# A graph layer and an eight-expert feed-forward layer on one core: 128-row blocks in pairs, five groups of tiles, biases inside the weights

## The reference, cut to what matters

```python
def _layernorm(x, axis=-1, eps=1e-05):
    m = jnp.mean(x, axis=axis, keepdims=True)
    v = jnp.var(x, axis=axis, keepdims=True)
    return (x - m) / jnp.sqrt(v + eps)
...
        h = layer_norm(x, ln_gamma, ln_beta)
        agg = jnp.einsum('bij,bjh->bih', adj, h)
        conv = jnp.einsum('bkh,ho->bko', agg, W_rel) + b_rel + jnp.einsum('bkh,ho->bko', h, W_root)
        return x + jax.nn.relu(conv)
...
        gate_scores = jnp.einsum('bsd,ed->bse', x, Wg) + bg
        topk_scores, topk_idx = jax.lax.top_k(gate_scores, K)
        topk_probs = jax.nn.softmax(topk_scores, axis=-1)
        combine = jnp.sum(topk_probs[..., None] * jax.nn.one_hot(topk_idx, E, dtype=x.dtype), axis=-2)
        out = jnp.zeros_like(x)
        for e in range(E):
            h = jax.nn.relu(jnp.einsum('bsd,hd->bsh', x, W1[e]) + b1[e])
            y = jnp.einsum('bsh,dh->bsd', h, W2[e]) + b2[e]
            out = out + combine[..., e:e + 1] * y
        return out
    x = x + _L0_gnn_ref(_layernorm(x, axis=-1), adj, L0_gnn_W_rel, L0_gnn_b_rel, L0_gnn_W_root, L0_gnn_ln_gamma, L0_gnn_ln_beta)
    x = x + _L0_ffn_ref(_layernorm(x, axis=-1), L0_ffn_Wg, L0_ffn_bg, L0_ffn_W1, L0_ffn_b1, L0_ffn_W2, L0_ffn_b2)
```

## Time and profile before

| | us |
|---|---|
| median of 3 runs | 629.91 |
| lowest and highest run | 625.02, 630.95 |
| span of the profiled execution | 878.1 |
| busy in it: PE, DVE, POOL, ACT | 471.1, 385.6, 272.6, 237.7 |

### The profile page before, as it was taken

The page is one execution under the profiler, slowest core; times in us unless marked ns, Lnnn a source line. Parts: engine busy times, 40 slices in busy tenths (PEclk is TensorE's granted clock), DMA queues, the critical chain, the costliest instruction groups (busy, mean ns, idle before and its releaser), DMA issues.

```text
span 878.1 us, 14976 instructions
## 1 busy us (share of the span) xinstructions
PE 471.1 (54%) x4776; PEld 395.1 (45%) x4777; DVE 385.6 (44%) x1146; ACT 237.7 (27%) x467; POOL 272.6 (31%) x268
## 2 busy tenths in 40 slices
PE   0613243441799997401099997201299951899500
PEld 0613233330688886201088886100188840688400
DVE  2979933830454667200044668000055620456622
ACT  0413100210356554000056553000044410344200
POOL 3053373067000000777400001777300067000274
PEclk9955575565799999655589999655599975899955
DMA  9980012011112112211112112111122222221341
GB/s 346 416 287 1 19 51 64 6 58 51 43 44 78 56 57 67 68 54 51 33 44 78 57 57 82 52 54 51 27 73 72 72 78 53 74 73 54 135 132 57
DMA packets 32173, 70.78 MB, mean 81 GB/s; under 512 B 14458, under 2 KB 14714, under 8 KB 31364
## 3 DMA queue, kind: packets, MB, share of 16 engines
q1 hardware_dynamic: 21520, 37.66, 13.0%
q0 software_dynamic: 8192, 16.79, 6.6%
q10 hardware_dynamic: 2420, 15.77, 4.4%
HBM read 32.45 MB, written 37.75 MB: 80 GB/s over the span
## 4 chain that ended last, share of the span: by engine, by line
PE 42%; issue 20%; another core or an unknown queue 13%; DVE 13%; DMA 4%; ACT 3%; POOL 3%; SPq 2%; ACTq 0%; DVEq 0%; POOLq 0%
PE PH L876 14%; PE PY L893 13%; PE PH L872 5%; POOL YG L311 3%; DMA ADJ<-in_adj 3%; PE PX L859 2%; ACT N L695 1%; PE PY L886 1%; SPq L223 1%; ACT N L677 1%; PE PA L824 1%; DVE VARN L377 1%; DVE MDIF L376 1%; DVE N L442 1%
## 5 line engine op out<-in xcount | busy, mean ns | idle before, releaser
L298 POOL DMA_INDIRECT rows<-XHL,IDX x128 | 123.2, 962 | 347.1 <-DVE IDX L515 309.3
L540 DVE SCALAR_TENSOR_TENSOR HL<-PH,HH 128x512 f16<-128x512 f32 x192 | 129.8, 689 | 207.0 <-ACT HH L726 114.1
L726 ACT ACTIVATE HH<-PH 128x512 f16<-128x512 f32 x192 | 113.6, 596 | 263.1 <-PE PH L876 107.9
L311 POOL DMA_INDIRECT YG<-yrows,IDX x128 | 121.3, 948 | 202.7 <-DMA yrows<-YB 164.3
L876 PE MATMUL PH<-XT,W1H 128*128 128x256 f16 x768 | 144.3, 281 | 22.8 <-issue 22.6
L893 PE MATMUL PY<-W2H,HL 128*128 x768 | 131.0, 223 | 31.8 <-issue 31.8
L893 PE MATMUL PY<-W2H,HH 128*128 x768 | 131.1, 223 | 25.3 <-issue 25.3
L893 PE MATMUL PY<-W2L,HH 128*128 x768 | 109.3, 223 | 42.1 <-issue 42.1
L535 DVE COPY XT<-PX 128x512 f16<-128x512 f16 x96 | 40.5, 422 | 168.6 <-issue 63.1
L876 PE MATMUL PH<-XT,W1L 128*128 128x256 f16 x384 | 107.8, 281 | 12.3 <-issue 12.3
L876 PEld LDWEIGHTS PH<-XT,W1H 128*128 x768 | 76.3, 100 | 55.8 <-issue 32.9
(11 more groups left out here) (154 smaller groups left out, 559.8 us busy)
## 6 DMA issues: line engine op xcount, KB each, us to landing
rows<-XB ACTq DMA_DIRECT2D x4, 3072.0 KB, 29.8
XB<-rows SPq DMA_DIRECT2D x32, 384.0 KB
yrows<-YB SPq DMA_DIRECT2D x32, 384.0 KB, 2.3
out<-X SPq DMA_DIRECT2D x16, 256.0 KB
X<-in_x SPq DMA_DIRECT2D x3, 1024.0 KB, 28.2
YG<-in_w ACTq DMA_DIRECT2D x1, 2048.0 KB, 9.6
ADJ<-in_adj SPq DMA_DIRECT2D x32, 64.0 KB, 3.8
YG<-in_w SPq DMA_DIRECT2D x1, 2048.0 KB, 29.7
```

What stands on the lines that cost most here:

```text
L298: nc.gpsimd.indirect_dma_start(rows[q], bass.IndirectOffsetOnAxis(ap=IDX[:, col:col + 1], axis=0), XHL[:, src:src + 2 * P].bitcast(F32), N ...
L311: nc.gpsimd.indirect_dma_start(YG[q % 2][:, dst:dst + P], None, yrows[q], bass.IndirectOffsetOnAxis(ap=IDX[:, col:col + 1], axis=0)).then_ ...
L540: nc.vector.scalar_tensor_tensor(HL[:, at:at + 2 * BW], PH[h][:, :], 0.0, HH[:, at:at + 2 * BW], ALU.max, ALU.subtract).then_inc((loa_made ...
L726: nc.scalar.activation(HH[:, at:at + 2 * BW], PH[h][:, :], ACT.Relu).then_inc((hia_made, hib_made)[h][j], 1)
```

## The change: what it does, and its diff

The whole kernel is written anew around the same arithmetic.

- Blocks have 128 rows. An expert's slots are padded to whole blocks of 128. Two blocks form a pair, and each block of a pair has its own expert number (two value_loads for each pair). A group of m tiles has 2m + 8 blocks.
- The tiles form five groups of 8, 16, 16, 16 and 8 tiles, with 24, 40, 40, 40 and 24 blocks: 168 blocks, 84 pairs, instead of 96 blocks of 256 rows.
- The hidden layer of a pair has 24 matmuls of 128 columns and no bias matmul; its output has 2 bias matmuls and 24 others, all of 128 columns.
- The bias b1 is folded into the weights: a normalised row sums to zero, so its last feature is replaced by a constant 1, every weight row has the last row subtracted, and the last row becomes the bias. b_rel, bg, gamma and beta are folded in the same way (AF, WF). residual is one DVE instruction instead of two.
- The weights are folded and split by PE and ACT: for each of 16 pieces of 512 columns PE multiplies in float32 (twice for W1, once for W2), ACT writes the high part, PE subtracts it, ACT writes the low part. POOL does no arithmetic any more.
- Graph quads 0 to 5 (groups 0 and 1) run before the first pair, in three lots of two. Quads 6 to 15 run between the pairs, each over six pairs from the one in START. Statistics, routing and combine have their pairs in STATS, ROUTE and COMBINE. Group 1 is routed in pairs 0 to 3.
- The order of POOL is scatter 0, 1, gather 0, scatter 2, 3, gather 1, scatter 4, gather 2, 3, 4, with 16 indirect DMAs for a group of 8 tiles and 32 for one of 16: 128 and 128 in all, as before.
- Nothing is in a loop of the hardware; all 84 pairs are written out on every engine. xT_copy is on ACT. ACT issues the stores of results. SP loads rows in chunks of 4 blocks into a ring of 4, and the adjacency tiles of later quads between these loads.
- Two row buffers are filled with zeros instead of four (2.6 MB each).

In the PE list, pair p is: rows_transpose(p+1), hidden(p), then xn_transpose or relation of a quad, output(p-1), then score, convolve or h0_transpose of a quad.

```diff
+GS = (8, 16, 16, 16, 8)
+G = len(GS)
...
+NS = [2 * s + E for s in GS]
+S0 = [sum(NS[:g]) for g in range(G + 1)]
+P0 = [s // 2 for s in S0]
+NP = P0[G]
...
+XR, YR = 4, 3
...
+START = {6: 2, 7: 5, 8: 8, 9: 11, 10: 15, 11: 19, 12: 23, 13: 27, 14: 32, 15: 37}
+STATS = {2: 0, 3: 9, 4: 27}
+ROUTE = {1: 0, 2: 17, 3: 33, 4: 43}
+COMBINE = {0: 24, 1: 26, 2: 60, 3: 62, 4: 64, 5: 66, 6: 78, 7: 80, 8: 82, 9: 83}
...
+            def load_rows(ch):
+                g, c = chunk_cols(ch)
+                if 2 * ch == P0[g]:
+                    sp.wait_ge(scattered[g], 2 * GS[g] * 16)
+                if ch >= XR:
+                    sp.wait_ge(xT_done, 2 * (ch - XR) + 2)
+                sp.dma_start(XB[:, ch % XR * CW:(ch % XR + 1) * CW], rows_p[g][:, c]).then_inc(xb_in[ch % XR], 16)
...
+            for ch in range(NC):
+                load_rows(ch)
+                for n, at in START.items():
+                    if ch == at // 2 + 2:
+                        sp.wait_ge(conv_done, n - 3)
+                        load_adj(n)
...
             scatter(0)
             scatter(1)
+            gather(0)
             scatter(2)
-            gather(0)
             scatter(3)
             gather(1)
+            scatter(4)
             gather(2)
             gather(3)
...
+            gather(4)
...
+            def residual(n):
+                dve.wait_ge(conv_done, n + 1)
+                dve.wait_ge(sum_made, n + 1)
+                xv = X[:, n * GW:(n + 1) * GW]
+                nc.vector.scalar_tensor_tensor(xv, banks(n)[0][:, :], 0.0, xv, ALU.max, ALU.add).then_inc(conv_read, 1)
+                dve.wait_ge(conv_read, n + 1)
...
+            for p in range(NP):
+                for n, at in START.items():
+                    if p == at + 5:
+                        split_low(n)
+                        scores(n)
+                    if p == at + 2:
+                        residual(n)
+                    if p == at + 3:
+                        scales_out_first(n, 1)
+                    if p == at + 4:
+                        scales_out_last(n, 1)
+                low_half(p, 0)
+                low_half(p, 1)
+                for n, at in START.items():
+                    if p == at + 2:
+                        stats_out(n, 0)
+                for g, at in STATS.items():
+                    for i in range(GS[g] // GT):
+                        if p == at + i // 2:
+                            stats_in(g, i)
+                    if p == at + 2:
+                        scales_in_first(g)
+                        scales_in_last(g)
+                for g, at in ROUTE.items():
+                    if p == at:
+                        route_first(g)
+                    if p == at + 1:
+                        route_second(g)
+                    if p == at + 2:
+                        route_slots(g)
+                        route_rows(g)
+                    if p == at + 3:
+                        route_blocks(g)
+                for n, at in COMBINE.items():
+                    if p == at:
+                        combine(n)
...
+            def weight_whole(c):
+                if c >= 3:
+                    pe.wait_ge(wlo_made, c - 2)
+                w = slice(c % E * HID, (c % E + 1) * HID)
+                if c < E:
+                    nc.tensor.matmul(WB[c % 3][:, :], KF[:, K_M:K_M + P], YG[0][:, w], start=True, stop=False)
+                    nc.tensor.matmul(WB[c % 3][:, :], KF[0:1, K_E:K_E + P], B1R[0:1, w], start=False, stop=True).then_inc(w_done, 1)
...
+                    nc.tensor.matmul(WB[c % 3][:, :], ident, YG[1][:, w], start=True, stop=True).then_inc(w_done, 1)
...
+                nc.tensor.matmul(WB[c % 3][:, :], KH[:, neg:neg + P], hi[:, c % E * HID:(c % E + 1) * HID],
+                                 start=False, stop=True, skip_group_check=True).then_inc(w_rest, 1)
...
+            def hidden(p, es):
+                pe.wait_ge(xT_made, p + 1)
...
+                    if p:
+                        pe.wait_ge((loa_made, lob_made)[h], p)
+                    for t in range(2):
+                        hi, lo = XT[:, at + t * P:at + (t + 1) * P], XT[:, at + BW + t * P:at + BW + (t + 1) * P]
+                        for c in (2 * h, 2 * h + 1):
+                            o = PH[h][:, c % 2 * BW + t * P:c % 2 * BW + (t + 1) * P]
+                            wh = W1H[:, bass.ds(es[t] * C + c * P, P)]
+                            wl = W1L[:, bass.ds(es[t] * C + c * P, P)]
+                            nc.tensor.matmul(o, wh, hi, start=True, stop=False)
+                            nc.tensor.matmul(o, wh, lo, start=False, stop=False)
+                            last = nc.tensor.matmul(o, wl, hi, start=False, stop=True)
+                    last.then_inc((ha_done, hb_done)[h], 1)
...
+            def output(p, es):
+                pe.wait_ge(loa_made, p + 1)
+                pe.wait_ge(lob_made, p + 1)
+                if p >= 2:
+                    pe.wait_ge(y_made, p - 1)
+                for t in range(2):
+                    py = PY[p % 2][:, t * P:(t + 1) * P]
+                    nc.tensor.matmul(py, KH[:, H_B2M:H_B2M + P], B2[:, bass.ds(es[t], P)], start=True, stop=False)
+                    for c in range(C):
+                        at = (p % 2 * C + c) * BW + t * P
+                        wh = W2H[:, bass.ds(es[t] * C + c * P, P)]
+                        wl = W2L[:, bass.ds(es[t] * C + c * P, P)]
+                        nc.tensor.matmul(py, HH[:, at:at + P], wh, start=False, stop=False)
+                        nc.tensor.matmul(py, HL[:, at:at + P], wh, start=False, stop=False)
+                        last = nc.tensor.matmul(py, HH[:, at:at + P], wl, start=False, stop=c == C - 1)
+                last.then_inc(y_done, 1)
```

More of the change, by code:

```diff
@@ L274, in _ @@
+            for n in range(NQ):
+                if n not in COMBINE or COMBINE[n] // 2 + 6 >= NC:
+                    store_out(n)
+            sp.wait_ge(out_done, NQ * 16)
         @block.gpsimd
@@ new lines, in _ @@
+            for n in (0, 1):
+                u_copy(n)
+            for n in (0, 1):
+                plus_norm(n)
+            split_weights(0)
+            for n in (0, 1):
+                split_high(n)
+            for n in (0, 1):
+                xnT_copy(n)
+            act.wait_ge(b2_zero, 1)
+            act.wait_ge(b2_in, 32)
+            nc.scalar.activation(B2[0:1, :], B2F[0:1, :], ACT.Copy, scale=YS / 64.0).then_inc(b2_made, 1)
+            nc.scalar.activation(BT[32:33, :], B2F[32:33, :], ACT.Copy, scale=YS / 64.0).then_inc(bt_made, 1)
@@ L810, in h0_transpose, with relation @@
                 last.then_inc(h0T_done, 1)
-            def relation(k, bank, there):
-                pe.wait_ge(hT_made, there)
-                for t in range(GT):
-                    last = nc.tensor.matmul(tile(bank, t), tile(T4, k * GT + t), WREL[:, :], start=True, stop=True)
+            def relation(n):
+                pe.wait_ge(hT_made, n + 1)
+                for k in range(GT):
+                    last = nc.tensor.matmul(tile(banks(n)[1], k), tile(quad(T4, n), k), WF[:, 0:P], start=True, stop=True)
@@ L817, in relation, with convolve @@
                 last.then_inc(u_done, 1)
-            def convolve(k, bank, there, loaded):
-                pe.wait_ge(u_made, there)
-                pe.wait_ge(adj_in[k], loaded)
-                for t in range(GT):
-                    nc.tensor.matmul(tile(bank, t), tile(T4, k * GT + t), WROOT[:, :], start=True, stop=False)
-                    last = nc.tensor.matmul(tile(bank, t), tile(ADJ, k * GT + t), tile(U4, k * GT + t), start=False, stop=True)
+            def convolve(n):
+                pe.wait_ge(u_made, n + 1)
+                pe.wait_ge(adj_in[n % 4], 32 * (n // 4 + 1))
+                for k in range(GT):
+                    o = tile(banks(n)[0], k)
+                    nc.tensor.matmul(o, tile(quad(T4, n), k), WF[:, P:2 * P], start=True, stop=False)
+                    last = nc.tensor.matmul(o, tile(quad(ADJ, n), k), tile(quad(U4, n), k), start=False, stop=True)
@@ L826, in convolve, with xn_transpose @@
                 last.then_inc(conv_done, 1)
[L828 to L831 removed]
+            def xn_transpose(n):
+                pe.wait_ge(xn_made, n + 1)
+                for k in range(GT):
+                    last = nc.tensor.transpose(tile(banks(n)[2], k), tile(quad(N4, n), k), ident)
                 last.then_inc(xnT_done, 1)
[L834 to L838 removed]
@@ new lines, in _ @@
+            nc.tensor.matmul(PA[:, 2 * P:2 * P + E], KF[0:1, K_E:K_E + P], KF[0:1, K_BG:K_BG + E], start=False, stop=True).then_inc(fold_done, 1)
+            pe.wait_ge(wf_made, 1)
+            for n in (0, 1):
+                h0_transpose(n)
+            for n in (0, 1):
+                relation(n)
+            for n in (0, 1):
+                convolve(n)
+            pe.wait_ge(w1_in, 16)
+            pe.wait_ge(b1_in, 16)
+            pe.wait_ge(kh_in, 16)
+            split_weights(0)
```

(20 more changed lines are left out.)

1286 lines of the change are left out of this document (617 added, 669 removed).

## The result

The changed kernel takes **670.85 us** (median of 5 runs, 664.52 to 675.8) against 629.43 for the kernel before beside it (5 runs): a ratio of **1.062**, with a 95% interval of 1.055 to 1.068. It is slower; 532 us was predicted, and the range ended at 585. A second time, on other runs, it took 665.06, ratio 1.056 (1.052 to 1.061). Some executions of a kernel are slower than its others at a lower granted clock (2 of the first 5 runs here, 1 of the second 5); medians are of all runs, ratios and intervals leave these out.

A forecast was written before the change was run, and what follows sets the result against it. PE's blocks were taken to pace the kernel before, POOL's queue to bound the changed one's end. The sum: 165 to pair 9's wait, plus 142.5 is 307.5, plus 201.6 is 509, end 520, with 12 carried over 532 us; range 492 to 585.

The forecast's parts named there:

- A pair: Each pair's work on PE without a quad: hidden matmuls at 0.056 us, the rest unchanged; 3.01 us, 84 pairs 253.
- Start: Everything before pair 0, with the first graph quads and weight folding: pair 0 at 95 us (bounds 86 and 112).
- pairs 0 to 3: First pairs, where DVE's added work holds PE back: 24.5 us including pipeline filling, slots of group 1 at 119.5.
- the new wait: In pair 9, PE's convolve(8) waits for an adjacency tile queued behind scatter 1's rows: 15 us, until 165.
- Quads between pairs: From pair 9 to group 3's slots in pair 35: 6.4 us a quad, 142.5 in all (bounds 123 and 175).
- POOL from there: From scatter 3 on, POOL issues 160 indirect DMAs and finds each input ready: 201.6 us, to 509; POOL bounds the end.
- The 12 us carried over: Unexplained gap between the kernel before's summed terms, 618, and its timed median, added to the forecast (bounds 0 and 25).
- The standstill: Five stretches in the kernel before's profile, all engines but POOL nearly still, 268.5 us: claimed absent from timed runs.
- Rival (d): Standstills beside POOL's trains of indirect DMAs belong to straight code, not the profiler: 713 us; chance 0.06.
- Rival (c): In the pairs, a 128-column product with weights from a register's address costs above 0.056 us: 565, at the bound 608; chance 0.12.
- (b): Graph and experts mesh better between pairs: DVE's additions hide and pair 0 is at 86; sum 504 us; chance 0.15.
- (e): No gain: DVE and ACT both fall behind in the pairs, 5.9 us for each of 84: 633 us; chance 0.03.

The follow-up runs named there:

- h1: The changed kernel with every slot on expert 0 (no loads, constant addresses), timed where the kernel before took 629.53: 537.16 us, ratio 0.853.
- e1: The changed kernel with every slot on expert 0 (no loads, constant addresses), timed where the kernel before took 880.14: 792.93 us, ratio 0.900.
- e3: The changed kernel with both loads per pair kept but unused and constant matmul addresses, where the kernel before took 880.14: 812.72 us, ratio 0.923.

## Why the prediction was wrong

| Step | predicted | changed kernel | pairs without a choice (h1) |
|---|---|---|---|
| first hidden product | 95 | 101.15 | 92.96 |
| scatter 1 begins | 119.5 | 128.92 | 119.83 |
| wait for the tile in pair 9 ends | 165 | 174.54 | 165.31 |
| scatter 3 begins | 307.5 | 353.62 | 319.85 |
| POOL's last DMA is issued | 509 | 657.8 | 521.7 |
| span | 520 | 669.0 | 533.0 |
| time | 532 | 670.85 | 537.16 |

**The step that failed is "A pair", 3.01 us.** It priced "24 matmuls of 128 columns" by L893's 0.056 and held that "the rest is unchanged". The columns were right to 0.01 us.
The term's size carries the miss. h1 takes it away and comes to 537 against 671, 134 us less. That is fewer than 84 x 2.8 = 235, since in h1 POOL's queue takes over as the bound at 320, as the prediction had it, and, as I read it (no run shows it by itself), since part of a pair's extra time lies beside waits that pairs with quads have anyway.

**Start, pairs 0 to 3, the new wait:** right where the stream isn't the bound (h1 within 2.1 us at each of the three), which is partly luck: e1, the same file, has its first hidden product at 109.03, h1 at 92.96. In the changed kernel they come 6 to 10 us later; what part of that is the stream in pairs 0 to 8 and what the start, which differed by 6 us between two traces of the changed kernel itself (101.15 and 107.53), I can't say. The price of the wait itself was 15; it measured 10.9 in h1 and 3.9 in the changed kernel.

**Quads between pairs:** from the wait to scatter 3, 142.5 predicted, 154.5 in h1 (319.85 - 165.31), inside the bounds of 123 to 175; 12 too few, which is most of what h1's span has over 520.

**POOL from there:** right in h1, wrong in the changed kernel. POOL waits 76.08 us before gather 3 and 22.69 before its last one, for results that PE hasn't made:

```profile
575.36 0.94 POOL L293 DMA_INDIRECT YG<-yrows,IDX  x1 [76.08 <-DMA yrows<-YB]
...
637.93 1.12 POOL L293 DMA_INDIRECT YG<-yrows,IDX  x1 [22.69 <-DMA yrows<-YB]
...
656.84 0.94 POOL L293 DMA_INDIRECT YG<-yrows,IDX  x1 [0.30 <-issue]
```

**The 12 us carried over:** around a span lie 1.9 us, not 12. The 10 too many and the 12 missing at the quads cancel, so that h1 comes as near to 532 as it does is luck in part.

**The standstill** was misread as the profiler's. It made no large error in the sum, since its stretches were taken out, but the expectation that the profile after would show them failed. Rival (d) fails too: they aren't tied to straight code, and none took part in the 671.

**Rival (c)** came closest: a product "whose weights come from a register's address costs more". Its mechanism was put in the product, and its bound, 0.11 us for each of 24, gave 608. The cost lies in the instructions ahead of the products and in the loads, in output as much as in hidden, and it has no bound in the products' own rows. **Rivals (b) and (e)** fall: ACT and DVE don't bound the pair, e1's 3.02 has the same work on them.

## What to carry to other kernels

Before splitting a product's block so that each half has its own run-time address, list what TensorE's stream gets per block: matmuls, register instructions, loads. Here 18 register instructions and one load per 256 rows were free behind 3.4 us of columns, and some twice that cost 2.8 us; the padding saved (84 pairs for 104 blocks) was worth less. When the trace shows an instruction that starts late and names a semaphore of another engine, and the gap is the same at each step, ask what stands ahead of it in its own stream. And before building on a profile, compare its span with the times: here they told of two conditions of the chip, of which one adds 250 us to the kernel before.

## What the runs showed that I had not expected

- A load of a register in TensorE's stream costs 0.61 to 0.67 us where the stream is the bound (two together 0.5 where no register instructions follow, e3), and no product starts meanwhile: the gap before hidden is 1.09 us with two loads and 2.00 with four.
- Register instructions cost 0.042 to 0.096 us each where the stream is the bound, and nothing in the kernel before, where products of 256 and 512 columns cover them.
- The 1.1 us at a loop's edge vanish when no expert is chosen, with the loop still there.
- The standstills: the same kernel at 793 and at 537 us (medians), with engines that wait up to 39.9 us for nothing the profile shows, while indirect DMAs are issued.
